# A decoder layer on one core: the last 128-column block of probabilities times values in each half as one plain fp32 product instead of three split ones

## The reference

```python
scores = jnp.einsum('bhtd,bhsd->bhts', q, k) * (1.0 / np.sqrt(HD))
scores = jnp.where(mask, scores, -jnp.inf)
att = jax.nn.softmax(scores, axis=-1)
out = jnp.einsum('bhts,bhsd->bhtd', att, v)
out = out.transpose(0, 2, 1, 3).reshape(B, T, H * HD)
return out @ wo
```

## Time and profile before

| | |
|---|---|
| median of 3 runs | 1127.64 us (1125.31 to 1128.38) |
| profiled execution | 1127.76 us |
| its span, first to last instruction | 1125.9 us |
| TensorE busy | 1098.1 us, 98% |
| mean granted TensorE clock | 0.996 |

### The profile page before, as it was taken

One profiled execution on the slowest core, in us unless ns is written; L12 is line 12 of the kernel. 1 busy time (PEld: TensorE's weight loads), 2 busy tenths in 40 slices (PEclk: granted clock), 3 DMA queues, 4 the chain that ended last, 5 costly groups with the idle time before them and its releaser, 6 DMA issues.

```text
span 1125.9 us, 19197 instructions
## 1 busy us (share of the span) xinstructions
PE 1098.1 (98%) x5310; PEld 930.7 (83%) x5310; DVE 890.3 (79%) x1530; ACT 647.9 (58%) x1165; POOL 855.2 (76%) x583
## 2 busy tenths in 40 slices
PE   7899999999999999999999999999989899999997
PEld 6788888888888888888888888888877787888886
DVE  6778887877777787878887888788888899866767
ACT  5656665666566666656665666665665564333333
POOL 1699779977997799789878978997877758444431
PEclk9999999999999999999999999999999999999999
DMA  6856555555555554556555655655554602211102
GB/s 204 231 143 155 131 141 148 141 140 144 153 137 143 140 149 130 140 143 157 141 143 153 161 135 143 150 152 139 144 142 113 168 20 69 62 57 56 37 19 75
DMA packets 155550, 144.86 MB, mean 129 GB/s; under 512 B 15488, under 2 KB 135808, under 8 KB 155520
## 3 DMA queue, kind: packets, MB, share of 16 engines
q1 hardware_dynamic: 143360, 124.57, 42.9%
q10 hardware_dynamic: 12160, 19.93, 6.1%
HBM read 37.49 MB, written 2.10 MB: 35 GB/s over the span
## 4 chain that ended last, share of the span: by engine, by line
POOL 38%; PE 32%; issue 19%; DVE 4%; DMA 3%; ACT 2%; SPq 1%; POOLq 1%; ACTq 1%; DVEq 0%
POOL qk_raw L566 9%; POOL PT_lo L592 8%; POOL rope_s L567 7%; PE ACC L1564 6%; PE ACC L1566 6%; PE ACC L1565 6%; POOL Q_lo L576 4%; PE S L1564 3%; PE S L1566 3%; PE S L1565 3%; POOL wq_lo L545 3%; POOL wo_lo L545 2%; POOL qk_raw L570 2%; DMA rope_s<-qk_raw 1%; PE S L1580 1%
## 5 line engine op out<-in xcount | busy, mean ns | idle before, releaser
L1140 DVE CUSTOM_DVE_ANT_0 S<-S,mask 128x128 f32<-128x128 f32 (+7 forms) x256 | 193.8, 757 | 151.8 <-PE S L1582 151.8
L774 ACT ACTIVATE probs<-S,neg_max 128x128 f32<-128x128 f32 (+7 forms) x256 | 189.2, 739 | 191.3 <-DVE neg_max L1140 187.6
L592 POOL TENSOR_TENSOR PT_lo<-PT_lo,PT_hi 128x896 fp32r<-128x896 f32 (+1 forms) x90 | 195.9, 2176 | 23.1 <-ACT PT_hi L781 23.0
L1153 DVE STREAM_TRANSPOSE turned<-probs 128x128 f32<-128x128 f32 (+7 forms) x256 | 197.5, 771 | 3.8 <-ACT probs L774 3.7
L1223 DVE SCALAR_TENSOR_TENSOR y<-ACC,row_rcp,y 128x512 f32<-128x512 f32 x256 | 176.2, 726 | 1.6 <-PE ACC L1566 1.5
L566 POOL TENSOR_TENSOR qk_raw<-qk_raw,cos_sin 128x512 f32<-128x512 f32 x76 | 125.3, 1649 | 68.1 <-DMA rope_s<-qk_raw 67.9
L781 ACT ACTIVATE PT_hi<-PT_lo 128x896 fp32r<-128x896 f32 (+3 forms) x155 | 157.0, 1013 | 30.5 <-DMA PT_lo<-turned 30.4
L1564 PE MATMUL ACC<-PT_hi,V_hi 128*128 128x512 f32 (+1 forms) x378 | 129.6, 343 | 5.3 <-POOL PT_lo L592 4.0
L1580 PE MATMUL S<-K_hi,Q_hi 128*128 (+4 forms) x380 | 130.9, 345 | 3.4 <-ACT probs L774 2.7
L1565 PE MATMUL ACC<-PT_lo,V_hi 128*128 128x512 f32 (+1 forms) x378 | 130.9, 346 | 0.0
L1566 PE MATMUL ACC<-PT_hi,V_lo 128*128 128x512 f32 (+1 forms) x378 | 130.6, 346 | 0.0
(11 more groups left out here) (265 smaller groups left out, 2576.9 us busy)
## 6 DMA issues: line engine op xcount, KB each, us to landing
PT_lo<-turned SPq DMA_DIRECT2D x248, 112.0 KB, 2.5
PT_lo<-turned SPq DMA_DIRECT2D x124, 208.0 KB, 4.0
rope_s<-qk_raw ACTq DMA_DIRECT2D x152, 128.0 KB, 3.7
PT_lo<-turned SPq DMA_DIRECT2D x124, 128.0 KB, 2.6
PT_lo<-turned SPq DMA_DIRECT2D x124, 80.0 KB, 2.3
wq_raw<-in_L_attn_wq_dram SPq DMA_DIRECT2D x32, 256.0 KB, 3.0
wo_raw<-in_L_attn_wo_dram SPq DMA_DIRECT2D x32, 256.0 KB, 4.0
V_stage<-in_L_ffn_down_w_t_dram SPq DMA_DIRECT2D x7, 512.0 KB, 3.5
```

Source lines behind the costliest of these rows:

```text
L592: nc.gpsimd.tensor_tensor(lo, lo.bitcast(F32), hi.bitcast(F32), ALU.subtract).then_inc(pt_lo_done[half], 1)
L774: nc.scalar.activation(dst, src, ACT.Exp, bias=neg_max[:, at:at + 1], scale=-1.0, accum_out=row_sum[:, j % 2, i:i + 1]).then_inc(exp_done, 1)
L1140: nc.vector.tensor_tensor_reduce(src, src, bias, scale=1.0, scalar=MASKED, op0=ALU.add, op1=ALU.min, accum_out=neg_max[:, at:at + 1]).then ...
L1153: nc.vector.transpose(dst.rearrange("p b (r i) -> p r b i", i=QB), src.rearrange("p (r b i) -> p r b i", b=4, i=QB)).then_inc(turn_done, 1)
```

## The change

The last key block of each half is computed as a single product of plain fp32 operands: the unsplit probabilities, which stay in `PT_lo`, and unsplit values in a new tensor `V_raw`, which holds the last block of each half. The splits of the probabilities leave that block out, and ScalarE fills `V_raw` from ACC ahead of the copy to `V_hi`.

```diff
-        V_stage = sb("V_stage", [T])
+        V_stage, V_raw = sb("V_stage", [T]), sb("V_raw", [2, HD])
...
+        def split_of(tensor, tiles):
+
+            half, at = tiles[0] // HT, tiles[0] % HT * PITCH[tiles[0] // HT]
+            if tiles[-1] % HT < HT - 1:
+                return of_tiles(tensor, tiles)
+            units = tensor[half][:].rearrange("p a (n i) -> p a n i", i=QB)
+            return units[:, :, at:UNITS[half] - 1, :].rearrange("p a r i -> p a (r i)")
+
+        def raw_of(tensor, half):
+
+            return of_tiles(tensor, range(half * HT + HT - 1, half * HT + HT), half * HT + HT - 1).bitcast(F32)
...
-                lo, hi = of_tiles(PT_lo, SENT[k]), of_tiles(PT_hi, SENT[k])
+                lo, hi = split_of(PT_lo, SENT[k]), split_of(PT_hi, SENT[k])
...
-                nc.scalar.activation(of_tiles(pt[0], SENT[k]), of_tiles(pt[1], SENT[k]).bitcast(F32),
+                nc.scalar.activation(split_of(pt[0], SENT[k]), split_of(pt[1], SENT[k]).bitcast(F32),
...
+                    nc.scalar.activation(V_raw[:, half], src[:, (HT - 1) * P:HT * P], ACT.Copy)
                 nc.scalar.activation(dst, src, ACT.Copy).then_inc(split_hi_done, 1)
...
+                        if k == count - 1:
+                            last = raw_product(acc, half, source[1])
+                            continue
...
+                    if k == NT - 1:
+                        last = raw_product(ACC[:, bank], 1, sources(j)[1])
+                        continue
...
+            def raw_product(acc, half, pt):
+
+                return nc.tensor.matmul(acc.rearrange("p (a u i) -> p a u i", a=4, i=QB)[:, :, HT - 1:HT, :],
+                                        V_raw[:, half], raw_of(pt, half), start=False, stop=True)
```

More of the change, by code:

```diff
@@ L645, in late_low @@
                 pool.wait_ge(pt_hi_done[half], heads * 3 + (k - 1) if half else heads * 2 + (k + 1))
-                hi, lo = [of_tiles(t, SENT[k]) for t in sources(j)]
+                hi, lo = [split_of(t, SENT[k]) for t in sources(j)]
                 nc.gpsimd.tensor_tensor(lo, lo.bitcast(F32), hi.bitcast(F32), ALU.subtract).then_inc(
@@ L1467, in _ @@
             dve.wait_ge(pt_hi_done[1], HEADS * 3)
-            hi, lo = [of_tiles(t, SENT[4]) for t in sources(REP - 1)]
+            hi, lo = [split_of(t, SENT[4]) for t in sources(REP - 1)]
             nc.vector.tensor_tensor(lo, lo.bitcast(F32), hi.bitcast(F32), ALU.subtract).then_inc(last_lo_done, 1)
@@ L1626, in other @@
                             pe.wait_ge(pt_lo_done[half], (n[f"pv{half}"] + 1) * (2 + half))
-                        pts = [of_tiles(pt, range(half * HT + first, half * HT + HT), k)
-                               for pt in ((PT_hi, PT_lo) if late is None else sources(late))]
+                        source = (PT_hi, PT_lo) if late is None else sources(late)
+                        if k == count - 1:
+                            last = raw_product(acc, half, source[1])
+                            continue
+                        pts = [of_tiles(pt, range(half * HT + first, half * HT + HT), k) for pt in source]
                         last = product(acc.rearrange("p (a u i) -> p a u i", a=4, i=QB)[:, :, first:, :],
-                                       [v[:, k, :] for v in (V_hi, V_lo)], pts, k == 0, k == count - 1)
+                                       [v[:, k, :] for v in (V_hi, V_lo)], pts, k == 0, False)
                 if end < count:
```

## The result

The changed kernel takes 1120.12 us (median of 5 runs, 1117.08 to 1122.99), the kernel before 1127.64 us (5 runs, 1125.31 to 1128.61). The ratio is 0.9936, with a 95% interval of 0.991 to 0.9962: 0.6% faster, 0.9 us from the 1121.0 us that I forecast. The changed kernel was run again in three later sets; over all 19 runs it lies between 1116.83 and 1122.99 us, with a median of 1119.70. So its span may not be compared with a median; only its parts may.

The account below looks back on a forecast made before the run. TensorE bounds the loop, partly VectorE and GpSimd near the end of attention. Plain product -5.4, lost to waits +0.9, narrower splits -1.8 and -0.3, copy nothing: -6.6, so 1121.0 us, 0.6% faster; range 1118.0 to 1126.5.

Parts of the forecast that it names:

- the sum of -6.6 us: Whole kernel: -5.4 + 0.9 - 1.8 - 0.3, giving 1121.0 us against the median of 1127.64.
- The plain product: Last block at 64 places on TensorE: 0.245 us instead of 0.33 for three split products, -5.4 us.
- my lower bound: Plain product on TensorE: 0.22 us if both records are held by the load alone, saving 7.0 us.
- What of it reaches the end: Loop and end of attention: all of TensorE's saving counts except before GpSimd's and VectorE's waits, +0.9 us.
- Six GpSimd waits at one place each: Loop, TensorE waiting for L592's low half: one place's saving lost at each, 6 x 0.085 = 0.5 us.
- half of eight places: Behind about 817 us, where VectorE's additions hold TensorE up: half the saving written off, 0.35 us.
- The narrower splits: Split groups of tiles 2 and 3 and of tile 7, 128 columns fewer: -1.8 us in the loop, -0.3 leaving attention.
- 0.3 at the end of attention: VectorE's last subtraction before TensorE's wait of 1.68 us: an eighth less of 2.17 us is 0.27, so -0.3.
- ScalarE's and VectorE's other savings at nothing: Narrower splits on ScalarE and VectorE elsewhere: they lie beside TensorE's work and count for nothing.
- the waits for L592's low halves: Sign in the new profile: TensorE's waits for GpSimd's low half of the probabilities below 0.2 us.
- The copy at nothing: ScalarE's 16 added copies to V_raw: hidden, counted at nothing; at most 7.7 us without cover.
- The rival of the clock: End of attention: with the 1.68 us wait at about 1.3 the clock may stay up, 1119.6 us; chance 0.12.

Follow-up runs that it names:

- the small kernel: Not the layer: only rows of split and plain products of each width, then pairs; plain products of 128 to 512 columns took 0.223, 0.43, 0.645 and 0.86 us.
- the first set: Runs beside before at 1126.48 us: the changed kernel again 1118.26, plain product with all columns split 1123.40, narrower splits with three split products 1122.68 us.
- full_splits: The changed kernel without its narrower splits, so all columns are split as before: 1123.40 us (0.9971 of before), in a later set 1123.22 us (0.9967).

## Why the prediction was right, and where it was not

The time was right (1121.0 against 1120.12 us, and 1119.70 over all runs), and so was its mechanism: a plain product is two records of two passes each, and TensorE sets the pace in the loop. But the sum of -6.6 us came so close by luck: two terms were too small on the side of gain, by 1.6 and 1.7 us, and one too small on the side of loss, by some 3.

- **The plain product.** I took 0.245 us, by the distance of 256-column split products; it costs 0.22, my lower bound. A record of the plain product has two passes, 0.107 us by the slope of the small kernel's rows, and the 0.12 of a split product of 256 columns holds a little more than its columns. What decided is that passes and load last about equally long at 128 columns. The term is -7.0 us, not -5.4.
- **What of it reaches the end.** Six GpSimd waits at one place each, and half of eight places, gave +0.9. Alone, the product saves 3.1 to 3.5 us of 7.0; so about 3.5 to 4 are lost. Behind the narrow splits it gives 4.4 us by the medians of the first set, 1122.68 to 1118.26, and 2.2 to 3.1 by the loop stretch. The step that failed is that I took the waits as six and as long as their idle column says. By distances between starts they are eleven in the loop, 4.37 us, and with the product sooner done they become 14. That does not account for all: in the loop 1.8 to 2.5 of 6.2 us are lost, 1.3 of them ahead of the two groups that I added up. Where the rest goes is open; the one trace of the kernel before is also 1.3 us slower than its median, so that stretches and medians can't be set against each other closer than that.
- **The narrower splits.** I took 0.3 us at each of six waits and 0.3 at the end of attention, -2.1. They are worth -3.8 us alone and -3.7 on top of the product (1123.3 to 1119.7 over all runs; 5.1 and 2.7 in the two sets). Again there are more waits than the six, and "ScalarE's and VectorE's other savings at nothing" failed: those of tile 7's group alone give 2.1 us by the medians, though the intervals still overlap. GpSimd's narrowed group itself was sized right (1.85 us).
- **The two halves together.** 3.1 and 3.8 make 6.9 us, and the three repeats of the changed kernel show 6.3 to 8.2. The wait that both work on was nearly used up: 4.37 us before, 1.5 after, while 0.74 ahead of the query projection became 1.4 to 2.9. That the waits for L592's low halves would be below 0.2 us was wrong too: 0.3 us was the longest in the loop by the idle column, 1.3 ahead of it, and 0.5 the longest in the loop for the query weights.
- **The copy at nothing.** Right: no engine waits for it, and leaving it out moved nothing. In the changed kernel the exponentials still wait for VectorE (186.5 us over the run on the page).
- **The rival of the clock.** It came true in the profiled execution, beside my forecast and not instead of it. The granted clock from 885 to 905 us was 0.91 before (us, then busy times, clock behind POOL's):

```profile
885.00:905.00 20.00, 17.37 (x103) 15.11 (x102) 16.64 (x31) 8.42 (x14) 13.63 (x6) 0.91 0.38 102
```

and 1.00 in the changed kernel:

```profile
885.00:905.00 20.00, 17.52 (x102) 15.01 (x103) 17.02 (x35) 5.87 (x12) 13.81 (x7) 1.00 0.25 73
```

Yet the wait ahead of it didn't shrink to 1.3 us, as I had made it depend on; the products behind it run at full clock all the same, 0.19 and 0.12 apart:

```profile
890.72 0.36 PE L1577 MATMUL ACC<-xT_hi,V_hi 128*128 128x256 f32 x1 [1.74 <-DVE xT_lo L1482]
890.91 0.28 PE L1578 MATMUL ACC<-xT_lo,V_hi 128*128 128x256 f32 x1
891.03 0.28 PE L1579 MATMUL ACC<-xT_hi,V_lo 128*128 128x256 f32 x1
```

Of the other three profiles of the changed kernel two stayed at 1.00, behind waits of 1.53 us, and so did `full_splits` behind 1.65; the one of the kernel before fell behind 1.68. The third fell to 0.91 too, but behind another and longer wait, just ahead of these products:

```profile
883.75 0.48 PE L1577 MATMUL ACC<-wo_hi,O_hi 128*128 128x512 f32 x1 [2.62 <-DVE y L1236]
```

Some 14 products of 256 columns then start 0.21 us apart instead of 0.12, which is 1.3 us; its stretch behind the loop lasted 72.49 us instead of 69.81 to 70.39, and the rest of that difference isn't the clock. Whether the kernel before always loses these 1.4 us, its one trace can't say, so how much of the measured gain is the clock stays open, and so does what decides it.

## What to carry to other kernels

At 128 columns with a weight load each, a split product costs its load, 0.11 us here; three of them can be replaced by one plain fp32 product at two thirds of the time, and at 256 columns no longer. Where TensorE waits again and again for a side engine's queue, shortening what that queue does can be worth as much as shortening TensorE's own work: 3.8 us against 3.1 here, and together about the sum. Of what the product saved on TensorE only some half reached the end, 3.1 to 4.4 of 7.0 us, with the narrow splits and without. Price such waits by distances between starts and not by the idle column, and look for the group behind the wait, where the rest of it turns up.

## What the runs showed of the hardware

A plain fp32 product of 512 columns takes 0.86 us, 3.8 times the 0.225 or so of a split one (102.20 to 102.43 in the earlier trace rows). "FP8 and Floating Point Precision" in the Trainium skill, section on TensorE precision notes, gives true fp32 four passes; the small kernel agrees, and adds that they come as two records with a load each.

GpSimd's instructions take longer beside VectorE's subtraction. GpSimd's low half of 896 columns takes two durations in the changed kernel's timeline of GpSimd,

```profile
406.28 3.65 POOL L604 TENSOR_TENSOR PT_lo<-PT_lo,PT_hi 128x896 fp32r<-128x896 f32 x1
411.14 2.15 POOL L578 TENSOR_TENSOR qk_raw<-qk_raw,cos_sin 128x512 f32<-128x512 f32 x1
...
418.35 1.29 POOL L578 TENSOR_TENSOR qk_raw<-qk_raw,cos_sin 128x512 f32<-128x512 f32 x1
...
431.89 2.69 POOL L582 TENSOR_TENSOR qk_raw<-qk_raw,rope_s 128x512 f32<-128x512 f32 x1
```

beside these rows of VectorE:

```profile
405.23 2.70 DVE L1173 TENSOR_TENSOR PT_lo<-PT_lo,PT_hi 128x1536 fp32r<-128x1536 f32 x1
411.08 1.04 DVE L1173 TENSOR_TENSOR PT_lo<-PT_lo,PT_hi 128x896 fp32r<-128x896 f32 x1
...
431.62 1.81 DVE L1173 TENSOR_TENSOR PT_lo<-PT_lo,PT_hi 128x1536 fp32r<-128x1536 f32 x1
```

Where a subtraction of VectorE lies beside it, the low half of 896 columns takes 3.65 us, against 2.12 in the earlier trace rows; the rotation product takes 2.15 instead of 1.29. VectorE's own 1536 columns take 2.70 us there and 1.81 at 431.62, and yet GpSimd is at work beside the latter too: its addition (L582) takes 2.69 us from 431.89, against 1.29 elsewhere (414.61). So at some places both lose, at others GpSimd alone; what decides it, no run shows. The "GPSIMD Engine Reference" in the Trainium skill, section on specifications, says that the two share their SBUF interfaces, with contention where a VectorE instruction has two SBUF inputs; these rows agree, as the subtraction has two.
